# Reordering the preparation of a graph layer with a mixture of experts behind it, on one core

## The reference, cut to what matters

```python
x = x + gnn(layernorm(x), src, dst, w, W1, W2, W3)        # x: 3125 x 256, 53125 edges sorted by dst
x = x + ffn(layernorm(x), gamma, beta, Wr, br, ...)       # 8 experts, the two best for each row

def gnn(x, edge_src, edge_dst, w, W1, W2, W3):
    agg = segment_sum(x[edge_dst], edge_src, num_segments=3125)
    y = agg + w * x
    h = relu(y @ W1.T); h = relu(h @ W2.T); h = relu(h @ W3.T)   # 256 -> 64 -> 32 -> 256
    return h + x
```

## Time and profile before

| | |
|---|---|
| time, median of 3 executions | 483.25 us (477.23 to 485.32) |
| span of the profiled execution, first to last instruction | 472.4 us (its own time is not listed beside it) |
| PE busy | 380.4 us, 81% |
| DVE busy | 294.7 us, 62% |
| ACT busy | 222.6 us, 47% |
| POOL busy | 135.4 us, 29% |

### The profile page before, as it was taken

How to read it: one execution, slowest core, us unless ns; L and a number is a source line. 1 busy time by engine, 2 the same in 40 slices (tenths; PEclk the granted TensorE clock), 3 DMA queues, 4 the chain that set the end, 5 groups by cost and what they waited for, 6 DMA issues and landing times.

```text
span 472.4 us, 12881 instructions
## 1 busy us (share of the span) xinstructions
PE 380.4 (81%) x4344; PEld 346.1 (73%) x4345; DVE 294.7 (62%) x704; ACT 222.6 (47%) x351; POOL 135.4 (29%) x241
## 2 busy tenths in 40 slices
PE   0895598999998889980449999999999999999200
PEld 0684498999998667770349999999999999999100
DVE  2886998999994753568945444445444444444853
ACT  2475576888885274560025444444444444443000
POOL 3050000000000500000054665665666665653200
PEclk9987589999999977875559999999999999999755
DMA  9620299999999269930011222212222222215899
GB/s 202 154 54 3 40 183 199 214 220 222 216 222 200 63 241 362 375 116 0 0 58 58 77 70 72 72 67 67 75 69 73 72 67 67 75 60 135 207 228 310
DMA packets 112696, 62.15 MB, mean 132 GB/s; under 512 B 86625, under 2 KB 106743, under 8 KB 112544
## 3 DMA queue, kind: packets, MB, share of 16 engines
q1 hardware_dynamic: 101168, 41.80, 36.6%
q0 software_dynamic: 6272, 14.93, 10.2%
q10 hardware_dynamic: 5232, 5.12, 3.7%
HBM read 27.70 MB, written 13.64 MB: 88 GB/s over the span
## 4 chain that ended last, share of the span: by engine, by line
PE 70%; DMA 9%; DVE 8%; ACT 5%; issue 4%; SPq 3%; POOL 0%; ACTq 0%; DVEq 0%; POOLq 0%
PE psum L918 20%; PE psum L929 19%; PE psum L790 9%; PE psum L781 7%; DMA w_sb<-pair_rows 3%; PE psum L837 3%; PE psum L859 3%; PE psum L907 2%; DMA at<-cts 2%; DMA b_rows<-in_L_ffn_b_dram 2%; PE psum L721 1%; DMA pair_rows<-yb,scol 1%; SPq L288 1%; PE psum L712 1%; ACT cts L591 1%
## 5 line engine op out<-in xcount | busy, mean ns | idle before, releaser
L918 PE MATMUL psum<-xgT,w_now 128*128 128x128 f32 x832 | 103.2, 278 | 0.0
L918 PEld LDWEIGHTS psum<-xgT,w_now 128*128 128x128 f32 x832 | 98.8, 195 | 0.2 <-issue 0.2
L929 PE MATMUL psum<-w_sb,hT 128*128 x416 | 98.4, 380 | 0.0
L591 ACT CAST cts<-psum 128x1000 bf16<-128x1000 f32 x100 | 78.4, 815 | 23.7 <-PE psum L781 23.3
L929 PEld LDWEIGHTS psum<-w_sb,hT 128*128 128x128 f32 x416 | 75.1, 190 | 8.3 <-issue 0.3
L679 ACT ACTIVATE hT<-up 128x512 f32<-128x512 f32 x52 | 32.8, 630 | 97.7 <-DVE up L1347 97.7
L790 PE MATMUL psum<-z,at 125*128 (+1 forms) x1875 | 71.0, 195 | 3.2 <-DMA at<-cts 3.2
L668 ACT COPY w_now<-w_sb 128x1024 f32 x52 | 54.4, 1046 | 34.5 <-DVEq L1312 21.9
L790 PEld LDWEIGHTS psum<-z,at 125*128 125x128 bf16 x1875 | 65.9, 100 | 3.8 <-DMA at<-cts 2.1
L1347 DVE TENSOR_TENSOR up<-psum,b1T 128x512 f32<-128x512 f32 x52 | 36.0, 692 | 47.8 <-PE psum L918 47.8
L492 POOL DMA_INDIRECT pair_rows<-yb,scol x52 | 52.0, 999 | 46.9 <-issue 33.6
(11 more groups left out here) (228 smaller groups left out, 347.8 us busy)
## 6 DMA issues: line engine op xcount, KB each, us to landing
w_sb<-in_L_ffn_W_dram SPq DMA_DIRECT2D x2, 4096.0 KB, 20.4
token_rows<-tok SPq DMA_DIRECT2D x5, 560.0 KB
tok<-pair_rows SPq DMA_DIRECT2D x5, 560.0 KB
w_sb<-pair_rows SPq DMA_DIRECT2D x5, 560.0 KB
out_dram<-res ACTq DMA_DIRECT2D x5, 560.0 KB
res<-in_x_dram ACTq DMA_DIRECT2D x3, 560.0 KB
res<-in_x_dram SPq DMA_DIRECT2D x2, 560.0 KB
b_sb<-in_L_ffn_b_dram SPq DMA_DIRECT2D x1, 1024.0 KB, 23.8
```

The lines of the kernel that those rows point to most:

```text
L591: act.copy(cts[:, par, :, d0:d0 + nw * WD].rearrange("p h (b d) -> p b h d", b=nb), psum[:, bank:bank + nb, 0:wb * WC].rearrange("p b (d h ...
L918: last = pe.matmul(psum[:, j % 2, c * P:(c + 1) * P], w1_now[:, j % 2, k, c * P:(c + 1) * P], xgT[:, j % 2, k, :], start=(k == 0), stop=(k ...
L929: last = pe.matmul(psum[:, 4 + j % 2, 0:D], hT[:, j % 2, k, :], w2_sb[:, ds(e, 1), k, :].rearrange("p a h -> p (a h)"), start=(k == 0), st ...
```

## The change

Eight things are done at once, all in the preparation or at its border.

1. The four small weights (`gW1_sb`, `gW2_sb`, `gW3_sb`, `b1_rows`) are issued from ACT's queue, ahead of ACT's loads of x. Before, SP issued them behind the edges.
2. PE's `crossing_rows` stands first of all on PE, ahead of the transposes of the weights.
3. DVE's check for sorted edges stands right behind `crossed`; the counting follows `kl_f`, and `start_f` and `start_i` follow the counting. `moments(0)` and all later ones come behind that.
4. PE turns one group more ahead of each first layer: `turn_x_rows(1)` now stands in front of `first_layer(0)`, `turn_x_rows(2)` in front of `first_layer(1)`, and so on.
5. ACT runs one Sqrt on a constant (`warm_act`) ahead of `hi_f`, so that one activation table serves the whole preparation.
6. ACT copies `xT` one group ahead, and casts the middle parts of all groups at the end.
7. `rest_of_hi` and `rest_of_mid` move from DVE to POOL, behind the gather. PE waits for them (`zsplit`) at the first `apply` and no longer ahead of the loop; ahead of the zeros it waits for `z_sb`, the five ACTIVATEs of each group, in place of `zhi`.
8. DVE makes `scale` behind its part of the loop and no longer ahead of it.

```diff
@@ sync
-            sp.dma_start(gW1_sb[:], gW1).then_inc(L["small"], 16)
-            ...
@@ gpsimd
             gather_edges()
+            def rest_of_hi(g):
+                grp = slice(g * G, (g + 1) * G)
+                pool.wait_ge(zhi, g + 1)
+                pool.tensor_tensor(zres[:, grp, :], z[:, grp, :], z3[:, grp, 0, :], ALU.subtract).then_inc(zrest, 1)
+            def rest_of_mid(g):
+                grp = slice(g * G, (g + 1) * G)
+                pool.wait_ge(zmid, g + 1)
+                pool.tensor_tensor(z3[:, grp, 2, :], zres[:, grp, :], z3[:, grp, 1, :], ALU.subtract).then_inc(zsplit, 1)
+            for g in range(NG):
+                rest_of_hi(g)
+            for g in range(NG):
+                rest_of_mid(g)
             pool.wait_ge(rounds_ready, 1)
@@ scalar
+            act.dma_start(gW1_sb[:], gW1).then_inc(L["small"], 16)
+            ...
             for g in (0, 2, 4):
                 load_x(act, g)
             act.wait_ge(c_pool, 12)
+            act.activation(std[:, 0:1], eps[0:T, :], ACT.Sqrt).then_inc(warm_act, 1)
             act.wait_ge(L["src"], 32)
...
-            for g in range(NG + 2):
-                if g < NG:
-                    copy_xT(g)
-                    deviation(g)
-                if 1 <= g <= NG:
-                    scale_z(g - 1)
-                if g >= 2:
-                    copy_mid(g - 2)
+            copy_xT(0)
+            act.wait_ge(warm_act, 1)
+            for g in range(NG):
+                if g + 1 < NG:
+                    copy_xT(g + 1)
+                deviation(g)
+                scale_z(g)
+            for g in range(NG):
+                copy_mid(g)
@@ tensor
             pe.wait_ge(c_dve, 1)
+            pe.wait_ge(crossing, 2)
+            for g in range(NG):
+                ...
             pe.wait_ge(gW1_centred, 1)
...
             turn_x_rows(0)
-            crossing_rows()
+            turn_x_rows(1)
             pe.wait_ge(c_act, 4)
             first_layer(0)
-            turn_x_rows(1)
             pe.wait_ge(rows_used, 1)
             pe.wait_ge(unsorted_dve, 1)
             pe.matmul(psum[:, 3, 0:1], ones[0:T, :], inv[:, 2:3], start=True, stop=True).then_inc(unsorted_pe, 1)
+            turn_x_rows(2)
             first_layer(1)
-            turn_x_rows(2)
             pe.wait_ge(start_dve, 1)
...
-            pe.wait_ge(zhi, NG)
+            pe.wait_ge(z_sb, NT)
             pe.wait_ge(rounds_ready, 1)
...
-            pe.wait_ge(zsplit, NG)
...
                         if kt >= 2:
+                            if c == 0:
+                                pe.wait_ge(zsplit, NG)
                             apply(kt - 2, 0, kt - 2, c)
@@ vector
             dve.tensor_copy(start_i[:], start_f[:, 0:NG]).then_inc(idx_ready, 1)
-            scales(1)
-            moments(2)
+            moments(0)
+            moments(1)
+            scales(0)
             dve.wait_ge(start_pe, 1)
...
             dve.tensor_reduce(largest_size[:], size_row[:], AX.X, ALU.max).then_inc(size_dve, 1)
+            moments(2)
+            scales(1)
+            moments(3)
             scales(2)
...
+            moments(4)
+            scales(3)
             dve.wait_ge(size_pe, 1)
...
             dve.tensor_copy(rounds_i[:], rounds_f[:, 1:2]).then_inc(rounds_ready, 1)
...
             scales(4)
...
             done, settle, start, st = chain(dve, link_late)
+            dve.wait_ge(rstd_ready, NG)
+            done(dve.tensor_scalar(scale[:, 0, :], rstd[:], 1.0, None, ALU.add))
+            done(dve.scalar_tensor_tensor(scale[:, 1, :], mv[:, :, 0], -1.0, rstd[:], ALU.mult, ALU.mult))
+            settle()
             dve.wait_ge(L["few"], 80)
```

More of the change, by code:

```diff
@@ L135, in build @@
         rounds_ready = sem("rounds_ready")
+        warm_act = sem("warm_act")
         gW1_centred, var_ready, std_ready, rstd_ready = sem("gW1_centred"), sem("var_ready"), sem("std_ready"), sem("rstd_ready")
@@ L358, in _ @@
             spread(sp, edge_i[:, 1, :], edges_of["src"], L["src"])
-            sp.dma_start(gW1_sb[:], gW1).then_inc(L["small"], 16)
-            sp.dma_start(gW2_sb[:], gW2).then_inc(L["small"], 16)
-            sp.dma_start(gW3_sb[:], gW3.rearrange("(a p) f -> p a f", p=P)).then_inc(L["small"], 16)
-            sp.dma_start(b1_rows[:], b1.rearrange("e (c p) -> (e c) p", p=P)).then_inc(L["small"], 16)
             sp.dma_start(next_i[0:T - 1, :], edges_of["dst"][1:T, 0:1], allow_slow_non_contiguous=True).then_inc(L["nextrow"], 16)
@@ L522, in _ @@
         def _(act):
+            act.dma_start(gW1_sb[:], gW1).then_inc(L["small"], 16)
+            act.dma_start(gW2_sb[:], gW2).then_inc(L["small"], 16)
+            act.dma_start(gW3_sb[:], gW3.rearrange("(a p) f -> p a f", p=P)).then_inc(L["small"], 16)
+            act.dma_start(b1_rows[:], b1.rearrange("e (c p) -> (e c) p", p=P)).then_inc(L["small"], 16)
             for g in (0, 2, 4):
@@ L692, in _ @@
             pe.wait_ge(c_dve, 1)
+            pe.wait_ge(crossing, 2)
+            for g in range(NG):
+                grp = slice(g * T, (g + 1) * T)
+                pe.matmul(psum[0:T, g, 0:EC + 1], crossed[:, grp], dst16[:], start=True, stop=True)
+                pe.matmul(psum[0:T, g, EC + 1:EC + 2], passed[:, grp], one16[:], start=True, stop=True).then_inc(rows_psum, 1)
             pe.wait_ge(gW1_centred, 1)
@@ L745, in _ @@
                       start=True, stop=True).then_inc(start_pe, 1)
+            turn_x_rows(3)
             first_layer(2)
-            turn_x_rows(3)
             pe.wait_ge(size_dve, 1)
             pe.matmul(psum[0:1, 3, 0:NG], largest_size[:], ident[0:NG, 0:NG], start=True, stop=True).then_inc(size_pe, 1)
+            turn_x_rows(4)
             first_layer(3)
-            turn_x_rows(4)
             first_layer(4)
-            pe.wait_ge(zhi, NG)
+            pe.wait_ge(z_sb, NT)
             pe.wait_ge(rounds_ready, 1)
@@ L980, in _ @@
             dve.tensor_tensor(crossed[:], begun[:], passed[:], ALU.subtract).then_inc(crossing, 1)
+            done(dve.tensor_tensor(junk[0:T, 0:EC - 1], dst16[:, 0:EC - 1], dst16[:, 1:EC], ALU.is_gt))
+            dve.wait_ge(L["nextrow"], 16)
+            done(dve.tensor_scalar(next_f[0:T - 1, :], next_i[0:T - 1, :], -float(HALF_RANGE), None, ALU.add))
+            settle()
+            done(dve.tensor_reduce(inv[:, 0:1], junk[0:T, 0:EC - 1], AX.X, ALU.add))
+            done(dve.tensor_tensor(inv[0:T - 1, 1:2], dst16[0:T - 1, EC - 1:EC], next_f[0:T - 1, :], ALU.is_gt))
+            settle()
+            dve.tensor_tensor(inv[:, 2:3], inv[:, 0:1], inv[:, 1:2], ALU.add).then_inc(unsorted_dve, 1)
             dve.wait_ge(L["small"], 64)
@@ L1004, in scales @@
                 dve.reciprocal(rstd[:, g * G:(g + 1) * G], std[:, g * G:(g + 1) * G]).then_inc(rstd_ready, 1)
-            moments(0)
             for g in range(NG):
@@ L1015, in _ @@
             dve.scalar_tensor_tensor(cnt[:, 2, :], psum[0:T, 0:NG, EC + 1], float(EC), cnt[:, 1, :], ALU.mult, ALU.add).then_inc(rows_used, 1)
[L1016 to L1026, removed]
             dve.wait_ge(unsorted_pe, 1)
@@ L1070, in _ @@
             dve.tensor_copy(rounds_i[:], rounds_f[:, 1:2]).then_inc(rounds_ready, 1)
[L1071 to L1074, removed]
             scales(4)
[L1076 to L1082, removed]
             dve.wait_ge(c_more, 7)
```

## The result

| | before | after |
|---|---|---|
| median of the timed runs | 480.68 us (477.23 to 485.32, 4 runs) | 489.90 us (487.18 to 491.71, 4 runs) |
| profiled execution's span | 472.4 us | 488.2 us (time 489.96) |
| X, start of the turn of the keys on PE | 43.46 us | 57.81 us |
| X to the end of the span | 428.9 us | 430.4 us |

The ratio after to before is 1.0229, with a 95% interval of 1.015 to 1.0308: slower; whether by more than 2%, the interval leaves open. (Ratios here leave out executions more than 1.5% slower than the quickest of their kernel, so they can differ a little from the quotient of two medians.) The two spans differ by 15.8 us, of which X holds 14.35.

A forecast was written before the change was run, and what follows sets the result against it. The z chain on PE was taken as the bound. `start_i` at 19.7 plus 19.55 + 4F, with F at 4.2 and zeros and transposes slower, gave X 57.4; less 1 us, 13 later, on the median 483.25: 496, range 486 to 502.

The forecast's parts named there:

- The ring: Preparation from `start_i` to X: PE, ACT and DVE hand work to each other, nothing hides it; 19.55 + 4F.
- Step 1: Behind `start_i` on DVE: `moments(0)`, `moments(1)` and `scales(0)`, 4.45 us.
- Step 2: ACT scales z of group 0, copies xT of group 2, PE's last transposes, then `first_layer(1)`: 2.5 + F.
- Step 3: PE turns `start_f`, DVE takes the sizes, then `moments(2)` and `scales(1)`: 3.9 us together.
- Step 4: ACT and PE again, with `scale_z(1)`, `copy_xT(3)` and `first_layer(2)`: 2.5 + F.
- Step 5: ACT and PE once more, with `scale_z(2)`, `copy_xT(4)` and two first layers: 2.5 + 2F.
- Step 6: End of preparation: last five ACTIVATEs 1.1, zeros 1.5, entering the loop 1.1; 3.7 us.
- the 1 us that I took off: Deduction from 13.9 us later at X, for part of one first layer at full clock; left 13.
- F: Time of one first layer on PE: 2.3 us at full clock, 4.2 expected at half clock.
- the 5.0 that I had at full clock: Rival for PE's preparation: clock stays at 1.00, X 48.45, 5.0 us later, 488 in all; chance 0.18.
- The edges land no earlier: Rival, edge loads: dst cast stays at 6.75, `start_i` 21.7, X about 58.5, 498; chance 0.06.
- this rival: POOL's split: subtractions delay first `apply` by 8 us (504) or hold up DVE's one-hots 4.5 us (500); chance 0.06.

The follow-up runs named there:

- both back: Changed kernel with moments back between the edge chain's steps on DVE and turns back behind the previous group's first layer on PE: 473.4 us, ratio 0.9865.
- PE's order alone: Changed kernel with moments and scales put back between the edge chain's steps on DVE, PE's turns left ahead: 474.5 us, ratio to before 0.9877.
- DVE's alone: Changed kernel with PE's turns put back behind the first layer of the group before, moments left behind `start_i`: 481.7 us, ratio 1.0088.
- The kept clock: Changed kernel with 26 and 16 unread matmuls in PE's pauses ahead of the last turns of groups 2 and 3: 485.0 us.
- the third profile of before: Kernel before, nothing changed, second of two further profiles: 480.69 us, X = 49.06.
- loads back: Changed kernel with the small weights on SP's queue again and x first on ACT's: 496.7 us.
- POOL busy: Changed kernel with 12 more subtractions on POOL ahead of the last of its split, beside DVE's one-hots: 495.8 us.

## Why the prediction was right, and where it was off

**The ring: right, step by step.** From `start_i` to X I had 36.75 and it took 37.13 (57.81 - 20.68). Step 1: 4.45 against 4.38 (20.68 to 25.06). Step 2: 6.7 against 6.92 (to 31.98). Step 3: 3.9 against 3.85 (to 35.83). Step 4: 6.7 against 6.94. Step 5: 10.9 against 11.2. Step 6: 3.7, and up to 1.1 for the zeros, against 3.9: the zeros did run slower, but the split of z no longer stands behind them. That the total agrees to 0.4 is in part luck: step 6 with its zeros was 0.9 too long, and the 1 us that I took off for a part of a first layer at full clock did not come. That the orders cause the loss is shown by the three runs that put them back. Counted from both back, PE's order alone costs X 2.8, DVE's alone 7.2, the two together 16.2. First layers above 2.3 us make up 2.3, 4.4, 7.1 and 7.9 of these four X (none, PE's, DVE's, both); without that, as an estimate in which nothing hides them, the orders cost 0.7, 2.4 and 10.6. So it takes DVE's order and PE's together, and either one back frees most of it.

**The clock: right in size, less simple in cause.** F was 4.30 against 4.2 from L859. Four first layers at 2.0 more are 8.0 of the 14.35, the zeros (1.68 between their first and second row, against 0.87) and three pairs of turns (0.68 against 0.43) some 1.5; 4.9 are left for the pauses and all else, against the 5.0 that I had at full clock. The kept clock, which gave 6.7 back for three layers and a bit, bears the division out. But I had the pauses lower the clock, and the third profile of before shows it lowered with PE busy 14.2 of 14.2 us. In all three profiles with the changed orders (this one, loads back, POOL busy) the four first layers behind the pauses took 4.3; without pauses it goes either way. Why one execution keeps the full clock and the next doesn't stays open.

**Edges and x.** The cast of dst came at 3.67; I took 4.8 between 2.8 and 6.75. The lower bound was misread: 2.8 is not the shortest landing on that page, `pair_rows` has 2.4. The sum of the check came at 19.49 against 18.7, since x landed at 12.4 where PE wanted it near 11; that was in the range. `start_i` ended at 20.68 against 19.7. "The edges land no earlier" is refuted.

**POOL.** Not late, by 13 us. The other half of this rival, that it holds up the one-hots, did not happen only because the five subtractions end 1.1 us before the first one-hot; I had said that they end about when those begin. The price that I gave it (4.5 us for five, 0.9 each) was the right order: with POOL kept busy it was 0.6 each. And in the run with both orders back POOL does cost 1.26, in an instruction I had not thought of.

**What was mis-sized: the base.** I forecast 496 and the median is 489.9, though X moved by 14.35 and I had 13. The step that failed is "I put the 13 us on the median": it took before's X as 43.46. That holds for the quick executions; in the one profile whose time (480.69) is that of the median, two first layers run at half clock and X is 49.06. The changed kernel has four of its five at half clock, so measured from such an execution its X is 8.75 later, near the 9.2 of the medians. I had seen that the executions of before differ by 8 us and used it for the width alone, where it said that the profile was not of the middle. The remaining 1.5 us lie behind X: in the changed kernel's profile the first third layer, for one, takes 4.61,

```profile
176.47 4.61 PE L854 MATMUL psum<-gW3T,h2T 128*125 128x256 f32 x10
```

where its counterpart in the profile of before takes 2.40 and in the third profile of before 4.61 as well, so the change is not needed for it. What makes up the 1.5 is not shown further; in the other runs, POOL busy apart, from X to the end takes 427.2 to 430.7.

## What to carry to other kernels

To move a critical-looking chain first is worth nothing where it was not the one that ended last, and everything put behind it pays: before such a move, write down which two engines were working beside each other at each step, and see whether they still are. Before a difference is put on a median, ask whether the profiled execution is a middle one; here the profile was some 6 us quicker than the median (its 472.4 against 478.7 in the third profile of before). And a new cost hidden by 1 us, as POOL's subtractions ahead of the one-hots, is hidden only until the next improvement.

## What the chip showed that I had not expected

The column of the granted clock shows 1.00 where the instructions run long. The run with moments back, PE's stretch from 12 to 31 (columns as above):

```profile
12.00:31.00 19.00, 18.64 (x86) 1.00 0.49 109
```

Two first layers in it take 4.30 each, as at 0.50 elsewhere. (Where the text says half clock of a layer under such a 1.00, its duration says so.) In the same way the crossing rows of the changed kernel take 0.59 to 0.60 each from 6.26 on, and the last of them in the kernel before, at 18.71, takes 0.37, with 1.00 shown for both stretches. The durations have to decide.

PE busy for 98% of 19 us stayed at the slower level there, while in the changed kernel the layer at 17.36, after 7.9 of 8.2 us, ran at the faster one. No run here shows what makes the difference.

An operation on one element on DVE took 1.41 us in place of 0.15 when POOL had just begun to subtract, and with POOL kept busy two operations on 125x5 took 0.56 and 0.71 in place of 0.16 and 0.17. Short instructions are not safe from POOL.
